# Two layers of convolution with preactivation on one core: a deeper pipeline between gather, interpolation and contraction, the residual by accumulating DMA, and a new weighting of the order

## What is computed

```
v   = samp(y0,x0)*(1-ly)*(1-lx) + samp(y0,x0+1)*(1-ly)*lx + samp(y0+1,x0)*ly*(1-lx) + samp(y0+1,x0+1)*ly*lx
out = einsum('bckhw,ock->bohw', v * sigmoid(mask), w)
```

## Time and profile before

| | us |
|---|---|
| median of three executions | 5774.03 |
| profiled execution, its own time | 5814.41 |
| its span, first to last instruction | 5812.6 |
| TensorE (PE) busy | 5111.7 |
| VectorE (DVE) busy | 4337.9 |
| GpSimd (POOL) busy | 2834.8 |
| ScalarE (ACT) busy | 2222.8 |

### The profile page before, as it was taken

How to read it: one execution, slowest core, us unless ns; L and a number is a source line. 1 busy time by engine, 2 the same in 40 slices (tenths; PEclk the granted TensorE clock), 3 DMA queues, 4 the chain that set the end, 5 groups by cost and what they waited for, 6 DMA issues and landing times.

```text
span 5812.6 us, 88098 instructions
## 1 busy us (share of the span) xinstructions
PE 5111.7 (88%) x31384; PEld 2834.8 (49%) x31448; DVE 4337.9 (75%) x11488; ACT 2222.8 (38%) x4640; POOL 2834.8 (49%) x2311
## 2 busy tenths in 40 slices
PE   7869998899888998889988999889998899886677
PEld 4535554455544554445544555445554455543333
DVE  4537888778887778868887787877788677876676
ACT  2234433344343443344433443333434334333343
POOL 0004545545455454554545454454545545446766
PEclk9979999999999999899999999999999999998888
DMA  2046778867787777867788677886768777777887
GB/s 94 26 161 218 242 239 303 291 230 254 240 302 265 253 244 275 302 222 260 240 278 310 229 236 249 288 299 218 261 230 317 266 244 245 258 268 273 311 308 270
DMA packets 493534, 1456.36 MB, mean 251 GB/s; under 512 B 45732, under 2 KB 115628, under 8 KB 492844
## 3 DMA queue, kind: packets, MB, share of 16 engines
q0 software_dynamic: 331776, 1208.11, 60.4%
q1 hardware_dynamic: 161324, 242.62, 11.8%
HBM read 1313.96 MB, written 136.59 MB: 250 GB/s over the span
## 4 chain that ended last, share of the span: by engine, by line
PE 58%; DVE 16%; issue 9%; ACT 6%; DMA 5%; POOL 4%; another core or an unknown queue 3%; SPq 1%; DVEq 0%; ACTq 0%; POOLq 0%
PE ps L678 23%; PE ps L711 7%; DVE V L1291 5%; PE ps L884 5%; PE ps L733 4%; PE ps L714 4%; PE ps L808 4%; POOL G L659 4%; DVE V L1286 3%; PE ps L821 3%; DVE E L1069 3%; PE ps L751 2%; PE ps L851 2%; DMA G<-table,IDX 2%
## 5 line engine op out<-in xcount | busy, mean ns | idle before, releaser
L659 POOL DMA_INDIRECT G<-table,IDX x2304 | 2833.8, 1230 | 2944.3 <-DVE V L1291 2016.7
L678 PE MATMUL ps<-VT,s_wconv 128*128 128x512 f32 x4608 | 2344.9, 634 | 201.4 <-ACT VT L1036 138.3
L1291 DVE SCALAR_TENSOR_TENSOR V<-G,WT,V 128x256 f32<-128x256 f32 x4608 | 1921.6, 480 | 0.0
L1036 ACT ACTIVATE VT<-ps 128x512 f32<-128x512 f32 x1152 | 686.3, 596 | 2700.5 <-PE ps L884 2180.7
L1286 DVE SCALAR_TENSOR_TENSOR V<-G,WT 128x256 f32<-128x256 f32 x2304 | 1015.8, 480 | 475.6 <-ACT G L1025 352.9
L678 PEld LDWEIGHTS ps<-VT,s_wconv 128*128 128x128 f32 x4608 | 845.1, 200 | 1042.2 <-issue 859.6
L1069 DVE TENSOR_TENSOR E<-ps,s_band 128x512 f32<-128x512 f32 (+1 forms) x1024 | 644.1, 673 | 454.0 <-PE ps L733 247.8
L884 PEld LDWEIGHTS ps<-s_ident,V 128*128 128x128 f32 x4608 | 588.1, 145 | 727.1 <-issue 702.5
L1025 ACT ACTIVATE G<-G,WT 128x256 f32<-128x256 f32 x1808 | 823.0, 501 | 244.6 <-DMA G<-table,IDX 225.8
L884 PE MATMUL ps<-s_ident,V 128*128 128x128 f32 x4608 | 714.0, 279 | 71.8 <-DVE V L1291 54.7
L711 PE MATMUL ps<-XN,s_wqk 128*128 128x512 f32 x1024 | 489.6, 605 | 34.1 <-issue 18.2
(11 more groups left out here) (102 smaller groups left out, 2947.4 us busy)
## 6 DMA issues: line engine op xcount, KB each, us to landing
table<-ACX SPq DMA_DIRECT2D x128, 528.0 KB
G<-table,IDX POOLq DMA_INDIRECT x2304
X<-in_x SPq DMA_DIRECT2D x64, 512.0 KB, 4.5
E<-in_x SPq DMA_DIRECT2D x128, 256.0 KB
x<-X SPq DMA_DIRECT2D x64, 512.0 KB, 6.7
R<-x SPq DMA_DIRECT2D x64, 512.0 KB
out<-R SPq DMA_DIRECT2D x64, 512.0 KB
s_wconv<-in_wconv SPq DMA_DIRECT2D x1, 2304.0 KB, 10.2
```

Of the source, the lines that this page charges most:

```text
L659: e.indirect_dma_start(G[a % NG][:, :], None, T[b % 2], bass.IndirectOffsetOnAxis(ap=IDX[b % 2][:, col:col + 1], axis=0)).then_inc(d_g[a % ...
L678: mm = e.matmul(CV[oh][:, :], s_wconv[:, h, t, oh * P:(oh + 1) * P], VT[U % 2][:, h, :], start=(t == 0 and h == 0), stop=(t == 8 and h == 1))
L1036: e.activation(VT[U % 2][:, :, 2 * P * pair:2 * P * (pair + 1)], BK[banks.place[use]][:, :].rearrange("p (h n) -> p h n", h=2), ACT.Copy). ...
L1291: e.scalar_tensor_tensor(vt[:, :], gt[:, q * C:(q + 1) * C], wt[:, col, q:q + 1], vt[:, :], ALU.mult, ALU.add).then_inc(lerp[q - 1], 1)
```

## The change

- The turn of pair m-2, not m-1, follows the lerp of pair m; V has 8 buffers, VT 3, G 11.
- `contract` of unit u-2 runs at the turns of unit u, first output half at pair 0, second at pair 1; four contractions are left at `conv.end`, where there were three.
- R is no longer loaded and added on VectorE. ScalarE copies CV into R; GpSimd issues a DMA that adds R into the output. x1 is stored in the output tensor, and the DRAM tensor X1 is gone.
- X is a ring of 5 slots in place of 8 buffers. The front loads x1 back from the output for the offset phase (`load_x1`).
- `pd` of a chunk stands one chunk ahead of `tp`; the links of `norm` and, for the last chunk, those of `mix` have three empty steps (HOP) between them; the weights are new.

```diff
-NX = 8
-NG = 10
-NV = 6
+NX = 5
+NG = 11
+NV = 8
+NVT_BUF = 3
+HOP = 3
+WEIGHT = {"st1": 5, "n.aggr": 2, "n.mean": 1, "n.dev": 4, "n.var": 1, "n.root": 1, "n.fin": 2,
+          "qkv": 6, "s": 5, "ext": 6, "lt": 3, "soft.max": 5, "soft.mix": 9, "soft.turn": 3, "sel": 5, "pv": 8,
+          "proj": 7, "proj.end": 8, "tp": 7, "om": 7, "ot": 4, "w.pos": 5, "w.mix": 11}
...
     def norm(j, b):
+        for kind in ("n.aggr", "n.mean", "n.dev", "n.var", "n.root", "n.fin"):
+            yield (kind, j, b)
+            yield from hop(HOP)
...
     def mix(b, c):
+        alone = HOP if c == NCH - 1 else 0
+        for kind in ("soft.max", "soft.exp", "soft.mix", "soft.turn", "soft.out"):
+            yield (kind, b, c)
+            yield from hop(alone)
...
     def offsets(b, c):
-        yield ("pd", b, c)
+        if c + 1 < NCH:
+            yield ("pd", b, c + 1)
+        if c + 5 < NCH:
+            yield ("load_x1", b, c + 5)
...
     def offset_phase(b):
         before = iter(())
+        yield ("pd", b, 0)
+        yield from hop(HOP)
...
-            steps.append(("turn", b, m - 1))
+            steps.append(("turn", b, m - 2))
...
+        def load_place(e, n, src):
+            if n >= NX:
+                b, v = divmod(n - NX, 2 * NCH)
+                if v < NCH:
+                    e.wait_ge(st2_done, 2 * (b * NCH + v + 1))
+                    e.wait_ge(*stored(b, v))
+                else:
+                    e.wait_ge(fill, b * NCH + min(v - NCH + 2, NCH))
+            e.dma_start(X[n % NX][:, :, :], src).then_inc(d_x[n % NX], 16)
...
# SP
+                elif kind == "load_x1":
+                    b, c = s[1:]
+                    e.wait_ge(*stored(b, c))
+                    load_place(e, place(b, c, True), chunk_of(out[b, :, :], c))
...
-                e.dma_start(X1[b % 2][:, :, c * CH:(c + 1) * CH], X[c][:, :, :]).then_inc(d_s[c], 16)
+                e.dma_start(chunk_of(out[b, :, :], c), X[k][:, :, :]).then_inc(d_s[k], 16)
...
# GpSimd
+                if kind in ("turn", "conv.end"):
+                    b = s[1]
+                    c, t = unit(s[2] // 2) if kind == "turn" else (NCH, 4)
+                    if c > 0 and t == 4 and (kind == "conv.end" or s[2] % 2 == 0):
+                        g = b * NCH + c - 1
+                        e.wait_ge(conv_out, 2 * (g + 1))
+                        e.wait_ge(*stored(b, c - 1))
+                        e.dma_start(chunk_of(out[b, :, :], c - 1), R[:, :, :], accum_op=ALU.add).then_inc(d_o, 16)
...
# TensorE
-                    if u > 1 and pair == 0:
-                        contract(1, b, u - 2)
-                    elif u > 0 and pair == 1:
-                        contract(0, b, u - 1)
+                    if u > 1:
+                        contract(pair, b, u - 2)
...
# ScalarE
+            def convolved(g, oh):
+                e.wait_ge(conv, 2 * (9 * g + 8) + oh + 1)
+                if oh == 0 and g > 0:
+                    e.wait_ge(d_o, 16 * g)
+                e.activation(R[:, oh, :], CV[oh][:, :], ACT.Copy).then_inc(conv_out, 1)
...
-                    if pair == 0 and U > 1:
-                        e.wait_ge(conv, 2 * (U - 1))
+                    if pair == 0 and U >= NVT_BUF:
+                        e.wait_ge(conv, 2 * (U - NVT_BUF + 1))
...
+                    c, t = unit(u)
+                    if c > 0 and (t, pair) in ((1, 1), (2, 0)):
+                        convolved(b * NCH + c - 1, 1 - pair)
...
# VectorE
-            def add_residual(g, oh):
-                c = g % NCH
-                last = (g // NCH) * UNITS + 9 * c + 8
-                e.wait_ge(conv, 2 * last + oh + 1)
-                if oh == 0:
-                    e.wait_ge(d_r, 16 * (g + 1))
-                e.tensor_tensor(R[:, oh, :], CV[oh][:, :], R[:, oh, :], ALU.add).then_inc(resid, 1)
```

More of the change, by code:

```diff
@@ L86, in order_of_steps, with hop @@
     offsets_run = [False]
+    def hop(n):
+        for _ in range(n):
+            yield IDLE
     def norm(j, b):
[L89 to L95, removed]
+        for kind in ("n.aggr", "n.mean", "n.dev", "n.var", "n.root", "n.fin"):
+            yield (kind, j, b)
+            yield from hop(HOP)
     def stats1(b):
@@ L133, in mix @@
                 yield ("sel", b, c, bank, hp)
-            yield IDLE
+            yield from hop(1 + alone)
             yield ("pv", b, c, hp)
@@ L160, in layer0 @@
                 yield ("load_x", b, c + 3)
+            if c == NCH - 1:
+                for n in range(3):
+                    yield ("load_x1", b, n)
             now = [mix(b, c)]
@@ L238, in order_of_steps @@
             done = fill(2 * m + 2, done)
+        steps.append(("turn", b, PAIRS - 2))
         steps.append(("turn", b, PAIRS - 1))
@@ L518, in k_view, with place, loaded, stored @@
             return KP[g % 3][:, :, :, :].rearrange("p h r w -> p h (r w)")[:, :, 0:CH]
+        def place(b, c, x1=False):
+            return 2 * NCH * b + c + (NCH if x1 else 0)
+        def loaded(n):
+            return d_x[n % NX], 16 * (n // NX + 1)
+        def stored(b, c):
+            n = place(b, c)
+            return d_s[n % NX], 16 * sum(v % (2 * NCH) < NCH for v in range(n % NX, n + 1, NX))
+        def load_place(e, n, src):
[7 more added lines that the diff above has]
+            e.dma_start(X[n % NX][:, :, :], src).then_inc(d_x[n % NX], 16)
         def chunk_of(t, c):
@@ L617, in _ @@
                         e.dma_start(dst, TT[:, :, :]).then_inc(d_t[half], 16)
[L618 to L625, removed]
-                        e.dma_start(chunk_of(out[b, :, :], done % NCH), R[:, :, :]).then_inc(d_o, 16)
-                    if kind == "turn" and t == 4 and pair == 0:
-                        g = b * NCH + c
-                        e.wait_ge(d_s[c], 16 * (b + 1))
-                        if g > 0:
-                            e.wait_ge(d_o, 16 * g)
-                        e.dma_start(R[:, :, :], X1[b % 2][:, :, c * CH:(c + 1) * CH]).then_inc(d_r, 16)
             e.wait_ge(d_o, 16 * NB * NCH)
@@ L974, in _ @@
                     need_pd_slot(e, b, c)
+                    for cc in range(0 if c == 0 else c + 1, min(c + 2, NCH)):
+                        e.wait_ge(*loaded(place(b, cc, True)))
                     for h in range(2):
@@ L1292, in _ @@
                                                    ALU.mult, ALU.add).then_inc(lerp[q - 1], 1)
-                elif kind == "turn" and s[2] >= 0:
-                    b, m = s[1:]
-                    u, pair = divmod(m, 2)
-                    c, t = unit(u)
-                    if t == 1 and pair == 0 and u > 8:
-                        add_residual(b * NCH + c - 1, 0)
-                    elif t == 1 and pair == 1 and u > 8:
-                        add_residual(b * NCH + c - 1, 1)
-                elif kind == "conv.end":
-                    for oh in range(2):
-                        add_residual((s[1] + 1) * NCH - 1, oh)
 def layouts(np, inputs):
```

59 lines of the change are left out of this document (25 added, 34 removed).

## The result

The changed kernel takes 5936.15 us (median of 4, 5919.3 to 5938.12), beside 5767.67 for the kernel before in the same runs: a ratio of 1.029, 95% interval 1.025 to 1.0329. On two other chips it was 1.0228 (1.0211 to 1.0245) and 1.0272 (1.024 to 1.0304). I had forecast 5626, faster. The profiled execution has a span of 5917.5 us.

A forecast was written before the change was run, and what follows sets the result against it. TensorE, busy 88%, was taken to wait on short chains, with VectorE and DMA limiting what the periods' second part could give back. Terms -165 + 35 - 10 - 8 = -148 gave 5626 us against the 5774.0 median; range 5490 to 5830.

The forecast's parts named there:

- Term 8: Boundary between images: first lerp ten us later, mostly covered by TensorE's qkv; 35 us on over seven, bounds 0 and 140.
- rival C: Boundary: gathers wait, then land behind the accumulate, first lerp 20 us later; 140 us on, 5868 in all; chance 0.15.
- Terms 1 to 6: Waits and clock of TensorE in the seven periods, mostly their second part: 183 us off, of which 165 counted.
- Terms 1 and 2: Front: `pd` one chunk ahead, and empty steps between group-norm links; 45 us of TensorE waits off for each.
- term 1: Front: `pd` made one chunk ahead of `tp`; 45 us off TensorE's 60.1 us wait for KP.
- Rival B: Periods' second part bound by VectorE and DMA, so closed TensorE gaps save no time there; 5763, chance 0.20.
- Terms 3 and 4: Convolution: later contraction on three VT buffers, 35 us off; later turn with eight V buffers, 18 us off.
- rival D: Convolution: buffers do not decouple because ScalarE copies, scales and stalls; 63 us less saved, 5689, within the forecast's 0.50.
- Term 5: Residual moved from VectorE to ScalarE: VectorE regains 11 us a period, ScalarE takes 10; no TensorE time by itself.
- Term 6: Clock in the periods' second part: with half its idle time gone, a third of 117 us returned, 40.
- Term 7: Residual traffic: accumulate issue 1.5 us, landing 7, extra read of 33.5 MB hidden; no cost in mid-image.
- Terms 9 and 10: Last convolution 10 us off, bounds 40 off and 20 on; prelude 8 us off.

The follow-up runs named there:

- the wait alone: Kernel before with one added wait: GpSimd holds the next image's first gathers until the last residual is added; 1.0211, 5720.65 us against 5596.62.
- the whole order: Kernel before with only the new weights, empty steps in norm and mix, and `pd` one chunk ahead; 0.9994, and 0.996 on a faster chip.

## Why the prediction was wrong, step by step

- **Term 8, the boundary, failed** at "TensorE's qkv covers it until T+18.6". I followed the wait of GpSimd to the gathers and to the lerp, and not through ScalarE: its next four instructions, the steps `scale(0)` and `scale(1)`, wait for those gathers, and behind them was XN, on which the cover itself depended. I took 5 us a boundary, 35 in all; the trace shows a gap of 14.8 and 2.8 more for the qkv at the lower clock behind it, some 108 us over six boundaries, and the wait alone costs 124. That lies inside the bounds of the term (0 to 140), but these were worked out from late gathers and not from a cover that fails. My rival C named the place, the sign and a price of 20 us, but its condition (gathers landing behind the accumulate) is not what happened: the first gather was issued at 3258.88 and its scale began at 3264.84, 6 us later, the usual landing, and at the six boundaries it was 5.7 to 7.7. That C came nearest to the time is in that part luck.
- **Terms 1 to 6, 165 us off, failed as a sum.** Terms 1 and 2 were about right on their rows (57 and 37 us of waits gone, 45 taken for each). But alone, term 1 is worth 0.5%, 21 to 27 us; the whole order 0 to 0.4%. When `pd` alone took 56 us of waits on KP away, some 28 to 35 us came back as waits for V. TensorE also waits for V, LS, CB and E, and a wait taken away mostly turned into another; the waits of one profile could not be added up as savings. The second part did not shrink (207.2 us beside 206.7, split by work).
- **Rival B** (nothing comes back) fits the time once the boundary is put right and the order of before is kept: 1.000 to 1.004, where B had 5763. Its reason, VectorE or the DMA engines at their limit, is not shown. In the part with norms and offsets VectorE is busy for 82% and the DMA share is 0.89, near the 90% that I had named as B's sign, but no run tests whether more traffic or less would move the time.
- **"The empty steps cost nothing while the whole fits in 144 pairs"** failed, but only beside the rest of the change: 1.5 to 2% there, nothing in the kernel before. The front ends at pair 133, near the 134 that I had counted, but the offset phase has 31 pairs and not the 34 or 35 that I wrote (35 before). Why this costs in one kernel and not in the other is open.
- **Terms 3 and 4, the depth**: nothing came of the 53 us. The wait on VT stayed at 62.5 us in the periods, in stalls up to 10 us, against the 4.8 us of slack that I had counted on. That is the outcome of rival D, which I had put inside the forecast. Its reason, that a ScalarE that stands still also stops the scales and so uses the slack up on both sides, is not shown by any run.
- **Term 5**: VectorE was relieved as forecast, 91 us in all, and no shorter stage goes with it: before, it was busy for 76% of the part with layer 0 and 83% of the rest, and now for 73% and 82%. It was not tried by itself.
- **Term 6**: I had counted on 40 us from a higher clock. The granted clock of the periods went from 0.97 to 0.96, with TensorE standing still more and not less, and fell to 0.70 to 0.77 for the first qkv behind each gap.
- **Term 7** held for what it covered: the accumulate's issue took 1.36 us (1.5 taken), and GpSimd waited for ScalarE 8 times, each at the end of an image, never in mid-image. The extra read of the destination shows nowhere in the counts: 1456.36 MB in all and 1313.96 MB read from HBM, in both kernels. The 33.5 MB more in the software queue (1241.67 for 1208.11) are the write of R, which left SP's queue (209.06 for 242.62). How long an accumulate takes to land has no row. The term left out ScalarE's copy as a step between two chunks, which costs 8 to 28 us in the last convolution here and 40 to 60 on faster chips.
- **Terms 9 and 10**: 10 off in the last convolution became 8 more (on faster chips some 40 to 60 more); the prelude's 8 became 2.

The sum as measured in steps on one of the slower chips, 1.0272 down: boundary 1.0%, order 1.3%, and 0.4% left for residual, ring and depth together. The shares hold for taking the parts out in this sequence: the same wait put into the kernel before costs 2.1%. Open is why the order and the ring cost together what neither costs without the other. The empty steps are the largest part. A second tile for the table and later loads of x1 seem to give some back too, but only by comparison across chips, and no part gives back all of it.

## What to carry over

When a wait is added on one engine, follow it through every queue, the one that feeds the supposed cover included: here the work that should have filled the gap was released by an instruction that itself stood behind the waiting ones. Waits of a bound engine read from one profile are not a sum that can be taken off; try the largest alone (`pd` ahead gained 0.5%) before building on all of them. A stage where the bound engine stands still can also cost behind the gap, in the clock. And empty steps in a paced order are not free by right: they cost nothing in one kernel and 1.5 to 2% in another, so try them where they will stand.

## What the hardware showed that I had not expected

The kernel before took 5765 to 5807 us on three chips and 5597 to 5619 on three others: some 3% apart, with each kernel steady on its chip. Where both kinds of chip have a trace of one kernel, the new order alone, nearly half of the difference lies in the last convolution: 529 us and 424. The traces show a difference that goes with it. On the slower chips ScalarE stands still before the copy into VT, 24 to 49 times and for up to 12 us, with no releaser on record ("remote" in the earlier trace rows); in the kernel before 47 times, 6 us on average. On the faster ones there is no such row at all. First the wait in the kernel before, then the copy into VT in the kernel with the added wait, on a faster chip, whose idle time is put down to TensorE alone:

```profile
ACT VT L1036 <- remote: 294.6, 47, 10.0
...
L1038 ACT ACTIVATE VT<-ps 128x512 f32<-128x512 f32 x1152 | 684.1, 594 | 2470.7 <-PE ps L886 2470.2
```

The Trainium skill ("Runtime: NRT & Kernel Launch", section "Instruction fetch mechanics") says that engines fetch instructions in blocks of 16 KiB over a DMA queue of their own and that this is mostly hidden. The profile of this case shows 254 packets and 4.16 MB on an instruction queue, which is 16 KB each, on both kinds of chips. Whether the stalls are these fetches, held up on some chips, no run here shows.

An accumulating DMA of 512 KB costs GpSimd 1.36 us of issue, 64 times out of 64 within 0.03 us. The gather issued behind it was not later than without one (5.7 to 7.7 us to its scale at six boundaries, beside 6.4 to 7.1):

```profile
L670 POOL DMA_DIRECT2D out<-R x64: 1332/1358/1382, 565.1 to 5909.5; - x64
```
